# Attention's loop: GpSimd splits the next head's row maxima behind the third tile's low part, where it did behind the first's

## What is computed

```python
def _attention(h, W_qkv, b_qkv, W_proj, b_proj):
    b, l, c = h.shape
    qkv = h @ W_qkv + b_qkv
    qkv = qkv.reshape(b, l, 3, H, D)
    q, k, v = (qkv[:, :, 0], qkv[:, :, 1], qkv[:, :, 2])
    scale = D ** (-0.5)
    scores = jnp.einsum('blhd,bmhd->bhlm', q * scale, k)
    attn = jax.nn.softmax(scores, axis=-1)
    o = jnp.einsum('bhlm,bmhd->blhd', attn, v).reshape(b, l, c)
    return o @ W_proj + b_proj
```

## Time and profile before

| What | Value |
| --- | --- |
| Median of three runs | 3061.78 us |
| Lowest and highest | 3058.14 and 3062.56 us |
| The profiled execution: its time | 3062.73 us |
| The profiled execution: its span, first to last instruction | 3061.1 us |
| Busy over the span: PE, DVE, POOL, ACT | 2805.0, 1680.9, 1437.3, 1416.8 us |
| Mean granted TensorE clock over the span | 0.959 |

### The profile page before, as it was taken

One profiled execution on the slowest core, in us unless ns is written; L12 is line 12 of the kernel. 1 busy time (PEld: TensorE's weight loads), 2 busy tenths in 40 slices (PEclk: granted clock), 3 DMA queues, 4 the chain that ended last, 5 costly groups with the idle time before them and its releaser, 6 DMA issues. The chain is left out here.

```text
span 3061.1 us, 51443 instructions
## 1 busy us (share of the span) xinstructions
PE 2805.0 (92%) x16066; PEld 2272.3 (74%) x16066; DVE 1680.9 (55%) x3417; ACT 1416.8 (46%) x1835; POOL 1437.3 (47%) x1073
## 2 busy tenths in 40 slices
PE   7859999969999999999999879689999999999977
PEld 3248878846666666666666568589999999999976
DVE  4446777558999999999999657511111111111126
ACT  2112322229999999999999836511111111111112
POOL 1232333128888888888888836512222222222210
PEclk8769999979999999999999989899999999999989
DMA  5476675653443434343343259892112111211126
GB/s 191 136 245 228 228 249 196 234 170 85 89 93 83 95 81 94 85 90 91 85 96 81 71 165 289 246 310 74 37 38 66 46 38 37 74 38 37 53 74 217
DMA packets 336907, 377.68 MB, mean 123 GB/s; under 512 B 162816, under 2 KB 226952, under 8 KB 336764
## 3 DMA queue, kind: packets, MB, share of 16 engines
q1 hardware_dynamic: 327162, 356.66, 39.0%
q0 software_dynamic: 4224, 9.44, 1.7%
q10 hardware_dynamic: 5382, 9.67, 1.0%
HBM read 225.77 MB, written 158.93 MB: 126 GB/s over the span
## 5 line engine op out<-in xcount | busy, mean ns | idle before, releaser
L896 POOL TENSOR_TENSOR a_pl<-a_pf,a_ph 128x1024 fp32r<-128x1024 f32 x384 | 908.6, 2401 | 24.8 <-ACT a_pf L1006 24.8
L929 DVE TENSOR_REDUCE a_mx<-a_psum_s 128x1 f32<-128x512 f32 x992 | 637.5, 684 | 92.4 <-PE a_psum_s L1035 88.5
L1004 ACT ACTIVATE a_ph<-a_psum_t 128x1024 fp32r<-128x1024 f32 x512 | 525.9, 1027 | 133.6 <-PE a_psum_t L1052 126.5
L1607 POOL TENSOR_TENSOR m_al<-m_af,m_ah 128x256 fp32r<-128x256 f32 x288 | 211.1, 733 | 760.1 <-DVE m_ah L1616 760.1
L1655 PE MATMUL m_psum_h<-m_ht,m_w 128*128 128x256 f32 x4032 | 528.1, 283 | 30.2 <-DMA m_w<-w_s 20.5
L1616 DVE CAST m_ah<-m_af 128x256 fp32r<-128x256 f32 x288 | 85.1, 295 | 830.2 <-ACT m_af L1593 830.2
L1655 PEld LDWEIGHTS m_psum_h<-m_ht,m_w 128*128 128x128 f32 x4032 | 504.3, 189 | 33.7 <-issue 32.9
L1593 ACT ACTIVATE m_af<-m_psum_h,m_bias 128x256 f32<-128x256 f32 x288 | 136.4, 473 | 826.7 <-PE m_psum_h L1655 826.7
L1669 PE MATMUL m_psum_y<-m_w,m_ah 128*128 128x288 f32 x2304 | 506.7, 295 | 1.6 <-DVE m_y L1633 1.5
L1071 PE MATMUL a_psum_o<-a_ph,a_vs 128*100 128x512 f32 x1024 | 420.9, 411 | 22.4 <-POOL a_pl L896 18.9
L1072 PE MATMUL a_psum_o<-a_pl,a_vs 128*100 128x512 f32 x1024 | 405.1, 396 | 0.0
(11 more groups left out here) (232 smaller groups left out, 3059.5 us busy)
## 6 DMA issues: line engine op xcount, KB each, us to landing
a_qs<-q_s SPq DMA_DIRECT2D x192, 144.0 KB
a_ks<-k_s SPq DMA_DIRECT2D x192, 144.0 KB
w_s<-q_ws SPq DMA_DIRECT2D x64, 324.0 KB, 3.5
h_s<-p_ht SPq DMA_DIRECT2D x40, 512.0 KB, 4.7
m_ht<-h_s SPq DMA_DIRECT2D x16, 1280.0 KB, 8.2
v_s<-q_vo SPq DMA_DIRECT2D x64, 288.0 KB, 2.3
a_vs<-v_s SPq DMA_DIRECT2D x128, 144.0 KB, 4.5
q_s<-q_qko SPq DMA_DIRECT2D x32, 512.0 KB, 2.7
```

Of the source, the lines that this page charges most:

```text
L896: pool.tensor_tensor(pl[:, s % RING], pf[:, s % RING], raw(ph[:, s % RING]), ALU.subtract).then_inc(lo_pool, 1)
L929: dve.tensor_reduce(mx[:, u % 2, t, h:h + 1], p_s[:, h * 512:(h + 1) * 512], AX.X, ALU.max) \
L1004: act.activation(ph[:, s % RING], p_t[:, s % 2], ACT.Exp, scale=SCALE)
L1607: pool.tensor_tensor(al[:, f % RING], af[:, f % RING], raw(ah[:, f % RING]), ALU.subtract).then_inc(lo_ready, 1)
```

## The change

One condition in POOL's loop: `split_max` is called behind step 2 of the eight, where it was called behind step 0. POOL has nothing in step 1 (DVE makes that low part), so one 128 x 1024 subtraction, that of tile 2, now stands ahead of the split. Nothing is added or removed, and no wait is different.

```diff
@@ -895,7 +895,7 @@
                             pool.wait_ge(exp_done, STEPS * hd + s + 1)
                             pool.tensor_tensor(pl[:, s % RING], pf[:, s % RING], raw(ph[:, s % RING]),
                                                ALU.subtract).then_inc(lo_pool, 1)
-                        if s == 0 and not (last and u == SLOTS - 1):
+                        if s == 2 and not (last and u == SLOTS - 1):
                             split_max(hd + 1, (u + 1) % SLOTS)
```

## The result

The changed kernel takes 3032.1 us (median of four runs, 3031.7 to 3035.3) against 3060.0 for the kernel before on the same chips. The ratio is 0.9913, with a 95% interval of 0.9896 to 0.9931, so it is faster by 21 to 32 us. Forecast were 3039 us and a range of 3032 to 3055: the direction and the mechanism were right, the size came out at the range's edge.

What follows compares the result with a forecast made beforehand. No single engine bounds the kernel; handovers lose time, with PE paying for POOL's wait. Per head -0.43 + 0 + 0.04 = -0.39 us, times 60 is 23.4 us off, giving 3039 us; range 3032 to 3055.

Steps and rivals of the forecast that it cites:

- POOL's wait was what PE paid for: POOL idles 2.1 us a head before the split; its late low parts cost PE 0.74 us a head.
- a chance of 0.03: Rival: PE regains all POOL waits, 0.9 us a head, 3008 us; chance of a result under 3032: 0.03.
- Steps 1 to 3 of the walk: PE's starts after DVE's transpose: `score_tile` 0.21 us earlier, `scores` of step 7 0.21, `values` of tile 4 0.43.
- the way of 2.91 us: From `score_tile` to the `scores` behind DVE's low part: a fixed 2.91 us, the same at two places in a head.
- It just fits: `score_tile`'s second matmul at 1211.05 needs DVE's reductions, which end at 1210.97, so it would not wait.
- step 1: On PE, `values` of tile 2 start without a wait, so `score_tile` of step 2 starts 0.21 us earlier.
- All stays as it is: From `values` of tile 4 to the next head's transpose nothing waits for POOL; the head is 0.43 us shorter.
- step 3: On PE, `values` of tile 4 start 0.56 us behind `scores` of step 7, at 1214.28 instead of 1214.71.
- The margin of the transpose: DVE's transpose at 1208.73 could start at 1208.65 after the later split: in time by 0.08 us, no wait.
- The landing: The maxima's DMAs delay `scores` of step 0 by 0 to 0.43 us in one head of four; 0.04 taken on average.
- The rival on the slower side: The split comes so late that DVE and then PE wait; slower from 0.51 us of lateness, chance 0.08.
- One for one beyond 0.08 us: At DVE's transpose, each us of split lateness beyond 0.08 us adds a us to each head.

Runs made afterwards that it cites:

- experiment 1: Kernel before, split left behind step 0 but taking the previous head's maxima, so POOL doesn't wait: 3028.1 us, ratio 0.9915.
- experiment 3: Changed kernel plus three small POOL copies ahead of the split, 0.38 us together: 3036.7 us, ratio 0.9935.
- experiment 4: Changed kernel with the maxima's DMAs issued on SP ahead of the second output store and gate rows: 3032.1 us, ratio 0.9932.
- experiment 5: Changed kernel with both three extra POOL copies ahead of the split and the maxima's DMAs issued early: 3027.4 us in one run.
- experiment 2: Changed kernel with the split moved one tile later, behind step 3: 3216.8 us in one run.
- experiment 6: Changed kernel with DVE's low part of tile 5 taken between the two reductions of score tile 2: 3051.6 us in one run.
- experiment 9: Fastest kernel (early maxima DMAs, score tiles of steps 2 and 6 interleaved with values, later transpose) with the split back behind step 0: 3042.7 us.
- experiment 10: The kernel before, profiled once more without any edit: 3057.8 us.

## Why the prediction was right, and where its sizes were off

- **POOL's wait was what PE paid for.** Right, and shown: taking away the wait alone gives the same head to within 0.001 us (experiment 1).
- **That the time lies in the range is luck.** The median, 3032.1 us, is 0.1 us above the lower bound of 3032, and two of the four runs lie below it, a region to which the prediction gave a chance of 0.03. The forecast time is 6.9 us too high: 4.5 because 23.4 us were forecast and 27.9 measured, 1.8 because the kernel before came out at 3060.0 where 3061.8 was used, and 0.6 by rounding up. The lower bound was low enough only because 4 us were taken off for the scatter of runs, not because the sum had a larger gain in it.
- **Steps 1 to 3 of the walk.** Predicted were 0.21 us at `score_tile`, 0.21 at `scores` of step 7 and 0.43 at `values` of tile 4; measured 0.20, 0.20 and 0.41. That the wait for POOL would be replaced by one for DVE, and the way of 2.91 us kept, was right. "It just fits", said of `score_tile` in step 1, was off by 0.08 us, the longer way from `score_tile` to `scores`; it cost nothing, because PE waited for DVE's low part right behind it.
- **"All stays as it is" behind step 3 was wrong by 0.06 us.** In the kernel before, the first `values` matmul of tile 4 took 0.47 us instead of 0.40, because it stood behind a wait. Between 900 and 1700 us all 143 of the L1071 matmuls that started over 0.3 us behind the matmul ahead took 0.47 to 0.48 us, and the other 620 took 0.39 to 0.40. I had counted this longer matmul for tile 2 and forgotten it here. By `scores` of the next step 0 the gain is 0.47, and an undisturbed head is 0.47 to 0.51 us shorter. This is the term that was mis-sized: 0.43 for 0.49.
- **The margin of the transpose.** Predicted 0.08 us, measured 0.07, and no wait.
- **The landing.** 0.04 us a head on average was forecast, from one head in four. It was one in four, with 0.22 us, so 0.06. The trace of the kernel before has the landing itself, in the increments of the semaphore that PE waits for: the last of them came at 1215.20 and 1232.44 us, 1.04 and 1.03 behind the end of the last issue, which is 1.65 behind its start. Against the weight load at 1232.28 that gives a wait of 0.16 us in that head, where the prediction had only bounds of 0 and 0.43. The Trainium skill ("DMA: Bandwidth & Descriptors", section "Anatomy of one DMA — SWDGE (gpsimd) path") puts the fixed part of a DMA at about 2.0 us, for DMAs that GpSimd issues; by it, as an estimate, that head would have waited 0.5 us, which is 0.13 on average (the prediction wrote 0.15). These four are issued by SyncE, and with 1.65 us the measurement decides against using the figure for them; what GpSimd's own DMAs take no run here shows.
- **The sum.** 0.43 us for a mean head of the loop, 25.0 us from the 4th to the 62nd transpose (972.5 to 947.5), and 2 us more in the first and the last heads, where 23.4 were forecast in all.
- **The rival on the slower side had the wrong price.** "One for one beyond 0.08 us" does not hold in general. For small delays it is too high: DVE has 0.28 us of idle time a few instructions later that takes most of the lateness up, and the landing pays more than the queue does (experiments 3 to 5). For a delay of 2.4 us it was right in the heads in which the clock stayed at 1.00 (2.43 us more); in two heads of three PE's pause also cost the clock, and the price was 3.39 (experiment 2).

What stays open: why the clock fell behind two of three pauses of equal length in experiment 2, and why the stages ahead of attention differ by up to 10 us between executions of one kernel. Experiments 2, 5, 6, 9 and 10 rest on one execution each; what is read from them is the head, 52 times in each profile.

## What to carry to other kernels

An engine that waits early for something it could take later is late for all that stands behind it; put ahead of the wait the piece of work whose input comes first, and place the waiting step just ahead of the moment at which its result is asked for. When such a wait goes, work out which tie is next by walking one period through the timeline, each start with what it waits for, and look for a way whose length stays the same at two places (here the 2.91 us): it tells how much comes back. A handover with a small margin isn't priced by its margin: look for idle time of the waiting engine a few instructions on, and for a DMA that hangs on the same step.

## What I had not expected of the hardware

- With a pause of 1.97 us on PE once in a head, the granted clock fell from 1.00 to 0.50 behind it in 36 of 52 heads, for 3.4 us each time, and stayed at 1.00 in the other 16; a fall cost 0.95 us. With PE's waits of 0.4 to 0.6 us, twice a head, it stayed at 1.00 from 900 to 1600 us.
- A `values` matmul that had to wait took 0.47 us where its neighbours took 0.40, in all 143 cases between 900 and 1700 us of the kernel before.
- Three 128 x 8 copies on POOL, which don't wait for each other, take 0.38 us together, where the split's two instructions, the second behind a semaphore of the first, lie 0.28 apart.
- A DVE wait of 0.27 us in each of 62 heads cost 0.06 us a head, because most of it came out of idle time that DVE had before a score tile.
